# A hybrid convolution, attention and expert kernel: the routed weights of the selection are laid out by their place modulo 4

## What is computed

```python
logits = jnp.einsum('bsd,ed->bse', x, gate_w) + gate_b
probs = jax.nn.softmax(logits, axis=1)                    # over the tokens
vals, idx = jax.lax.top_k(probs.transpose(0, 2, 1), K)    # 8 tokens of each expert
...
pooled = jnp.einsum('bked,bke->bed', gathered, topv)      # one vector per image and expert
...
weighted = jnp.einsum('beo,bke->bkeo', out, topv).reshape(Bn, K * E, O)
outputs = outputs.at[jnp.arange(Bn)[:, None], flat_idx].add(weighted)
```

## Time and profile before

| | us |
|---|---|
| three runs | 402.58, 408.36, 410.03 |
| median | 408.36 |
| the profiled execution | 402.22 |
| its span | 400.3 |
| TensorE busy (matmuls) | 348.1 |
| VectorE busy | 306.9 |
| ScalarE busy | 258.9 |
| GpSimd busy | 239.5 |
| mean granted TensorE clock | 0.944 |

### The profile page before, as it was taken

How to read it: one execution, slowest core, us unless ns; L and a number is a source line. 1 busy time by engine, 2 the same in 40 slices (tenths; PEclk the granted TensorE clock), 3 DMA queues, 4 the chain that set the end, 5 groups by cost and what they waited for, 6 DMA issues and landing times.

```text
span 400.3 us, 7849 instructions
## 1 busy us (share of the span) xinstructions
PE 348.1 (87%) x3046; PEld 260.0 (65%) x3046; DVE 306.9 (77%) x558; ACT 258.9 (65%) x347; POOL 239.5 (60%) x141
## 2 busy tenths in 40 slices
PE   1299999999899999999599999999986887979775
PEld 1188867667687676757477677686764545646675
DVE  3777879777969878699769786986998995766621
ACT  1132453897987959698476788898696887832500
POOL 5234454386678798787635989756497975153000
PEclk9999999999999999999799999999998997998755
DMA  4810000000000000000000000000020000000311
GB/s 142 169 25 1 2 2 0 3 2 0 3 2 2 2 0 3 2 1 2 0 2 2 2 2 2 2 2 2 0 55 1 3 0 25 19 0 2 106 53 52
DMA packets 16193, 6.93 MB, mean 17 GB/s; under 512 B 6767, under 2 KB 16029, under 8 KB 16157
## 3 DMA queue, kind: packets, MB, share of 16 engines
q1 hardware_dynamic: 13440, 5.78, 5.5%
q10 hardware_dynamic: 2717, 0.66, 1.1%
HBM read 3.63 MB, written 2.11 MB: 14 GB/s over the span
## 4 chain that ended last, share of the span: by engine, by line
PE 57%; DVE 15%; ACT 10%; issue 9%; DMA 4%; POOL 3%; ACTq 1%; SPq 0%; DVEq 0%; POOLq 0%
PE psB L912 13%; PE psA L912 11%; PE psB L1028 5%; ACT Pp L602 5%; PE psA L1013 4%; PE psB L1049 4%; PE psA L1095 3%; DVE negmax L770 3%; PE psA L902 3%; PE psA L1057 3%; PE psA L1073 2%; DVE Pp L395 2%; DMA x_all<-in_x_dram 1%; POOL Pp L395 1%; DVE xin L713 1%
## 5 line engine op out<-in xcount | busy, mean ns | idle before, releaser
L395 POOL TENSOR_TENSOR Pp<-e,Pp 128x1024 f16<-128x1024 f32 x45 | 107.4, 2393 | 11.7 <-ACT Pp L602 11.5
L770 DVE TENSOR_REDUCE negmax<-psA 128x1 f32<-128x512 f32 (+7 forms) x128 | 90.7, 750 | 18.3 <-PE psA L1016 17.6
L601 ACT ACTIVATE e<-psB 128x1024 f32<-128x1024 f32 (+1 forms) x80 | 76.6, 957 | 9.9 <-PE psB L1031 4.6
L602 ACT ACTIVATE Pp<-psB 128x1024 f16<-128x1024 f32 (+1 forms) x80 | 76.8, 960 | 0.0
L912 PE MATMUL psB<-xin,UU 128*128 128x224 f16 (+1 forms) x480 | 56.3, 276 | 1.1 <-ACT Pp L602 0.6
L1013 PE MATMUL psA<-zK,yQ 128*128 128x512 f16 (+1 forms) x192 | 49.1, 339 | 9.1 <-DVE uT L790 4.9
L912 PE MATMUL psA<-y,DD 128*128 128x224 f16 (+1 forms) x480 | 55.1, 273 | 0.0
L1028 PE MATMUL psB<-yQ,zK 128*128 128x512 f16 (+1 forms) x192 | 49.1, 335 | 6.9 <-ACT Pp L602 3.5
L912 PEld LDWEIGHTS psB<-xin,UU 128*128 128x128 f16 x480 | 46.7, 99 | 9.8 <-ACT oT L606 1.5
L912 PEld LDWEIGHTS psA<-y,DD 128*128 128x128 f16 x480 | 46.8, 98 | 5.5
L481 POOL TENSOR_TENSOR zrstd<-zrstd,power 128x8 f32<-128x8 f32 x16 | 26.3, 1643 | 29.9 <-DVE zrstd L750 29.6
(11 more groups left out here) (164 smaller groups left out, 602.6 us busy)
## 6 DMA issues: line engine op xcount, KB each, us to landing
x_all<-in_x_dram SPq DMA_DIRECT2D x4, 512.0 KB, 4.1
out_dram<-x_all SPq DMA_DIRECT2D x8, 256.0 KB, 2.3
yQ<-rows SPq DMA_DIRECT2D x32, 2.0 KB
Pp<-filter_tables ACTq DMA_DIRECT2D x4, 121.9 KB, 4.2
w_halves<-y SPq DMA_DIRECT2D x12, 32.0 KB, 1.8
cst<-shape_constants SPq DMA_DIRECT2D x1, 326.5 KB, 4.2
y<-in_L_ffn_weight_dram SPq DMA_DIRECT2D x4, 64.0 KB, 2.1
xin<-in_L_ffn_weight_dram SPq DMA_DIRECT2D x1, 256.0 KB, 3.5
```

The source lines that it names most:

```text
L395: return engine.tensor_tensor(Pp[:, n % 2, 1, o:o + N], e32[:, (NU * n + i) % 3, 0:N], Pp[:, n % 2, 0, o:o + N], ALU.subtract)
L601: nc.scalar.activation(e32[:, m % 3, 0:N], slot(e)[:, 0:N], ACT.Exp)
L602: nc.scalar.activation(Pp[:, n % 2, 0, UOFF[e[2]]:UOFF[e[2]] + N], slot(e)[:, 0:N], ACT.Exp).then_inc(b_drained, 1)
L770: ins = nc.vector.tensor_reduce(negmax[:, n % 2, m - 1:m], s[:, at:at + P * m], X, ALU.max, negate=True)
```

## The change

VectorE writes the routed weights in another order of columns. Before, token 4 q + r of an image stands in column 4 q + r. After, it stands in column 256 r + q: all tokens with the same place modulo 4 lie together. The instruction still takes its inputs in natural order; its three operands are now seen as 256 by 4, and neighbours in the output are 256 elements (1 KB) apart. by_tile then returns a contiguous block of 128 columns for each tile, for the transposes of "wT" and for the matmuls of "scatter". The values in wT and in the products are the same as before. No instruction is added or left out, and none changes its place in the order of its engine.

```diff
                 elif name == "route":
 
                     dve.wait_ge(p_scaled, n + 1)
-                    nc.vector.scalar_tensor_tensor(out=xF_all[0:GE, n, :], in0=rest[:, :], scalar=NEG, in1=probs[:, :],
-                                                   op0=ALU.is_equal, op1=ALU.mult).then_inc(route_ready, 1)
+                    def natural(v):
+                        return v.rearrange("p (q r) -> p q r", r=R)
+
+                    nc.vector.scalar_tensor_tensor(out=xF_all[0:GE, n, :].rearrange("p (r q) -> p q r", r=R), in0=natural(rest[:, :]),
+                                                   scalar=NEG, in1=natural(probs[:, :]), op0=ALU.is_equal, op1=ALU.mult).then_inc(route_ready, 1)
...
             def by_tile(v):
 
-                w = v.rearrange("p (a q r) -> p a r q", a=2, r=R)
-                return lambda k: w[:, k // R, k % R, :]
+                return lambda k: v[:, 2 * P * (k % R) + P * (k // R):2 * P * (k % R) + P * (k // R) + P]
```

## The result

| us | before | after |
|---|---|---|
| median of 20 runs each | 403.14 | 406.38 |
| lowest, highest | 401.51, 410.78 | 402.14, 408.75 |
| ratio after to before | | 1.0068, interval 1.0044 to 1.0092 |
| profiled execution | 402.22 | 405.91 |
| span of it | 400.3 | 404.1 |

A forecast was written before the change was run, and what follows sets the result against it. TensorE was taken to bound most of the kernel (57% of the chain), VectorE some (15%). The tail's -1.8 us and the earlier groups' +0.5 gave -1.3, from 408.36 to 407.1 us, range 400.3 to 410.2.

The forecast's parts named there:

- The routing write: VectorE's write of routed weights, four times: scattered output makes each +0.87 us longer, from 0 to 1.7.
- Transposes: TensorE's four groups of 8 transposes of xF_all: contiguous weights save 0.13 us a group.
- Scatter: TensorE's four groups of 16 scatter matmuls: contiguous weights save 1.9 us at full clock, 0.4 us at half.
- the weights load no faster: Rival: the scatter's 240 ns are not due to strided weights, the tail gains nothing; 410.1 us and slower, chance 0.08.
- The tail: Last part of the kernel: scatter, write and transposes sum to -1.75 + 0.87 - 0.13 - 0.4 - 0.4 = -1.8 us.
- The clock comes back in the tail: Rival: contiguous weights let TensorE's clock rise in the tail; -3.4 us more, total -4.7, 403.7 us, chance 0.14.
- Group 0: First group's routing write: VectorE's 1.15 us gap ahead of L765 takes in the 0.87 us, cost 0.
- group 2: Third group's routing write: followed by VectorE gaps of 0.60 and 0.95 us, cost 0.
- Group 1: Second group's routing write: delays maxima and yQ, for which TensorE waits at the transposes at 282.97 us; +0.87 us.
- something of the clock elsewhere, of either sign: Remaining case: TensorE's clock changes outside the tail, making the kernel faster or slower; no size given, chance 0.08.
- The sum: Whole kernel: tail -1.8 us and the three earlier groups +0.5 us give -1.3 us.
- the scattered write costs more than the reads give: Rival: routing writes each costing above 1.3 us more make the kernel slower; at 1.7 us, +1.7, 410.1 us, chance 0.15.

The follow-up runs named there:

- w2: Contiguous reads everywhere, new write only in the third group, against contiguous reads with the old write everywhere (398.95 us): median 399.20 us, ratio to before 0.9920.
- w1: Contiguous reads everywhere, new write only in the second group, against contiguous reads with the old write everywhere (398.95 us): median 405.94 us, ratio to before 1.0061.
- stall1: Contiguous reads, old write everywhere, one extra contiguous VectorE instruction of about 0.74 us ahead of the second group's routing write: median 406.63 us, ratio to before 1.0058.
- the fillers: Unused matmuls in TensorE's waits: four in the changed kernel, 402.96 us; four and twelve in both kernels, 402.09 us before and 400.74 changed.
- the tile order: Against the kernel before, uT copied contiguously as it stands in PSUM, no scattered write, contiguous reads: 399.30 us, ratio 0.9878; with both fillers 398.05 us.

## Why the prediction was wrong

- *The routing write*, +0.87 us taken from the copy of uT: 0.75 measured. Right in kind, a little too large.
- *Transposes*, -0.13 us a group: -0.46 measured at full clock (groups 0, 1 and 2), -0.10 in the tail at half clock (1.19 to 1.09). I compared them with those of u, which move 128 columns where these move 64, so the array's own time stood in for the gain that the weights could give. A term mis-sized by a factor of 3.5 where it ran at full clock.
- *Scatter*, -1.9 us at full clock and -0.4 at half: 4.00 to 2.05, and 4.02 to 3.72. Right. The rival that the weights load no faster is out.
- *The tail*, -1.8 us with its steps (the copy of uT late next, the pause of about 5 us): -1.8 measured.
- *The clock comes back in the tail*: it did not. Scatter 0 at 3.72 us and the pooling at 3.67 ran at half clock, with contiguous weights too.
- *Group 0*, 0 by way of the gap ahead of L765, and *group 2*, 0: w2 at 399.20 us against 398.95 bears out the second. Group 0 was not tried alone; in the trace of after its L765 starts at 205.22 instead of 205.06, and the transposes behind it no later than before.
- *Group 1*, "Queued behind the write are the maxima and yQ, and TensorE waits for them: +0.87": the right place and mechanism, +0.67 directly. This is the step that failed. I priced the wait as the time that it adds and put all that follows from it at nothing: the clock was kept as it was in the one profiled execution, and so was the order of VectorE's cast and GpSimd's L395. w1 shows 7 us in the median for this write alone, stall1 7.7 for another instruction of about its length, and the fillers take the loss back. How the 6 to 7 us beyond the direct 0.67 divide between the lower clock and the cast's wait is not measured. I gave "something of the clock elsewhere, of either sign" a chance of 0.08, and looked for the clock only in the tail.
- *The sum*: -1.3 us was forecast; with the clock held by fillers it is -1.35. That the two agree is partly luck: the write was smaller and the transposes' gain larger than forecast, which would give -1.5 to -2.5, and the runs do not show where the rest went. The same sum without the fillers has the other sign.
- *The rival "the scattered write costs more than the reads give"*, slower from a price of 1.3 us: the sign was right, its reason not. The price was 0.75, below its threshold.

I also read the spread of the three runs as noise that only sets the width of the range. The profiled execution was shorter than all three: that was the sign that one trace shows only one of several courses of the clock.

## What to carry to other kernels

Where TensorE waits for VectorE between two busy stretches, price a delay there twice: the delay, and what half clock would make of the stretches behind it. Before weighing fractions of a microsecond, look at the mean clock of several executions and not at one trace; if the times come in groups with the clock, first cover the longest pauses with matmuls whose result nobody uses, and judge the change with the clock held. Look also for an instruction that now starts behind one of another engine that it used to precede, as the cast here. A layout change is best pushed back to where a reordering copy exists already and can be dropped, as in the tile order.

## What the runs showed of the hardware

- An fp32 scatter record whose weights stand 16 bytes apart starts every 240 ns at either clock; with contiguous weights (4.00 - 0.40)/15 became (2.05 - 0.27)/15 = 119 ns at full clock and about (3.72 - 0.42)/15 = 220 ns at half, if one record at half clock takes some 0.42 us. The strided load was the bound, and the array's clock had been hidden beneath it.
- For the transposes (64 moving columns) the gain is smaller in proportion: 8 went from 1.17 to 0.71 us at full clock, where a scatter went from 4.00 to 2.05. The price of a 16-byte step is therefore not one figure for 128 columns of weights: 8 transposes that read them so start about (1.17 - 0.28)/7 = 127 ns apart, the scatter's records 240.
- VectorE writing fp32 with 1 KB between neighbours takes 1.96 us for 1024 columns; with 16 bytes between them out of PSUM (another instruction) 2.06 us. Contiguous, they take 1.21 and 1.22, so the extra of the two steps is nearly the same, 0.75 and 0.84. The Trainium skill, Vector Engine (DVE) Microarchitecture Reference, section The SBUF access granule: adjacent pairs, gives 1.71 ns a column for a write that hops 4 KiB at each element and 2.50 for one that steps 24 words, against 1.054 contiguous: 0.66 and 1.45 ns more. The 1 KB hop here costs (1962 - 1208)/1024 = 0.74 ns a column more than contiguous, near the first and far from the second.
- A cast of VectorE (16x128, fp32 to 16 bits, 0.22 us) that came behind the start of a GpSimd instruction of 2.13 us took 1.30 to 1.79 us in seven traces and ended some 0.08 us after it; where the cast started first, in seven others, it took 0.21 or 0.22.
- The same program ran with mean granted clocks from 0.919 to 0.944 and times from 401.5 to 411.6 us, on one core of each of three chips, with the best group present on all of them. What places the falls in one execution and not in the next stays open: the traces show where they come, not why this pause counts and that one doesn't. The clock stayed at 0.50 in the tail through 380 to 386 us of before, where TensorE was busy all the time.
